# A one-core transformer layer: four engines' loops run four iterations a turn in place of two

## What is computed

```python
h = _L0_tok_ref(L0_tok_log_dt, x, L0_tok_B, L0_tok_inv_A_real, L0_tok_A_imag, 1024)      # (64, 128, 1024)
h = jnp.concatenate([jnp.broadcast_to(cls_tok, (h.shape[0], 1, h.shape[2])), h], axis=1)
h = h + _L0_attn_ref(_layernorm(h, axis=-1), ...)
h = h + _L0_ffn_ref(_layernorm(h, axis=-1), ...)

# inside _L0_attn_ref, with h of width 128
h = gelu(x @ w_down.T + b_down)          # exact gelu
xmid = h
h = _hydra(h, *hp); h = _hydra(h, *hp)
h = xmid + (alpha * xmid + (1.0 - alpha) * h)
return x_init + (h @ w_up.T + b_up)

# inside _L0_ffn_ref
base_out = x @ base_W.T + base_b
w = top-8 softmax weights of x @ router_W.T + router_b, mapped to 8 experts
lora = ((x @ A) * w) @ Bm * 2.0
```

## Time and profile before

| | us |
|---|---|
| median of 3 runs | 2546.23 |
| lowest, highest | 2546.2, 2549.94 |
| the profiled execution | 2549.21 |
| its span, first to last instruction | 2547.5 |

### The profile page before, as it was taken

How to read it: one execution, slowest core, us unless ns; L and a number is a source line. 1 busy time by engine, 2 the same in 40 slices (tenths; PEclk the granted TensorE clock), 3 DMA queues, 4 the chain that set the end, 5 groups by cost and what they waited for, 6 DMA issues and landing times.

```text
span 2547.5 us, 52475 instructions
## 1 busy us (share of the span) xinstructions
PE 2236.7 (88%) x14117; PEld 1838.9 (72%) x14117; DVE 1993.2 (78%) x5213; ACT 1529.7 (60%) x2926; POOL 1038.7 (41%) x1365
## 2 busy tenths in 40 slices
PE   1136799999999999999999999999999999999998
PEld 1125577777777777777777777777777777777776
DVE  6846788888878788888888787888888888878664
ACT  3435576666666666666666666666666666666652
POOL 2634444444444344444444343444444443434321
PEclk9966699999999999999999999999999999999999
DMA  3211011111111111111111111111111111111211
GB/s 102 71 34 33 33 52 37 59 58 58 58 38 49 58 58 58 55 31 58 58 58 58 38 49 58 58 58 55 32 58 58 58 58 38 49 58 57 63 36 31
DMA packets 90062, 132.62 MB, mean 52 GB/s; under 512 B 20379, under 2 KB 63559, under 8 KB 90006
## 3 DMA queue, kind: packets, MB, share of 16 engines
q1 hardware_dynamic: 79176, 125.60, 16.6%
q10 hardware_dynamic: 10830, 6.35, 0.9%
HBM read 55.17 MB, written 76.74 MB: 52 GB/s over the span
## 4 chain that ended last, share of the span: by engine, by line
PE 35%; DVE 23%; issue 21%; ACT 12%; DVEq 2%; POOL 1%; ACTq 1%; DMA 0%; SPq 0%; POOLq 0%
PE bank L1457 8%; PE bank L1556 5%; DVE sp_x L1129 3%; DVE NF L1192 3%; DVE NF L1198 3%; PE bank L1661 3%; PE bank L1546 3%; ACT T L877 3%; ACT CX L892 2%; DVE W L1157 2%; ACT SQ L975 2%; DVEq L47 2%; PE bank L1512 2%; PE bank L1487 2%; PE bank L1499 2%
## 5 line engine op out<-in xcount | busy, mean ns | idle before, releaser
L1457 PE MATMUL bank<-w_hi,XHI 128*128 128x512 f32 (+1 forms) x1560 | 629.2, 403 | 1.4 <-DVE XLO L1348 1.4
L1457 PE MATMUL bank<-w_lo,XHI 128*128 128x512 f32 (+1 forms) x1560 | 554.3, 355 | 0.0
L1457 PE MATMUL bank<-w_hi,XLO 128*128 128x512 f32 (+1 forms) x1560 | 553.9, 355 | 0.0
L1095 DVE SCALAR_TENSOR_TENSOR CX<-bank,cw,CX 128x252 f32<-128x252 f32 (+5 forms) x804 | 342.9, 461 | 100.8 <-ACT CX L892 100.8
L877 ACT ACTIVATE T<-bank 64x512 f32<-64x512 f32 x256 | 151.8, 593 | 352.8 <-PE bank L1546 348.2
L1457 PEld LDWEIGHTS bank<-w_hi,XLO 128*128 128x128 f32 x1560 | 295.6, 189 | 46.4
L1457 PEld LDWEIGHTS bank<-w_hi,XHI 128*128 128x128 f32 x1560 | 296.5, 190 | 38.3 <-DVE XLO L1348 1.7
L1457 PEld LDWEIGHTS bank<-w_lo,XHI 128*128 128x128 f32 x1560 | 296.3, 190 | 38.1
L849 POOL TENSOR_TENSOR CB<-CB,CM 48x252 f32<-48x252 f32 (+5 forms) x402 | 267.6, 666 | 137.9 <-ACT CM L877 109.2
L792 POOL TENSOR_TENSOR NB<-GB,sp_dt 128x512 f32<-128x512 f32 x67 | 100.3, 1496 | 297.4 <-DVE GB L1175 297.4
L813 POOL TENSOR_TENSOR RS<-VE,half_neg 128x1 f32<-128x1 f32 x65 | 35.6, 547 | 409.7 <-DVE VE L1292 409.7
(11 more groups left out here) (296 smaller groups left out, 5786.9 us busy)
## 6 DMA issues: line engine op xcount, KB each, us to landing
carried<-T SPq DMA_DIRECT2D x65, 512.0 KB, 4.7
T<-carried SPq DMA_DIRECT2D x65, 512.0 KB, 3.9
out<-HB SPq DMA_DIRECT2D x129, 256.0 KB, 3.2
tables<-tab SPq DMA_DIRECT2D x8, 560.0 KB, 4.1
TB<-tables SPq DMA_DIRECT2D x64, 70.0 KB, 2.8
carried<-U SPq DMA_DIRECT2D x65, 64.0 KB, 3.6
XM<-carried SPq DMA_DIRECT2D x65, 64.0 KB, 4.7
XI<-in_x SPq DMA_DIRECT2D x128, 32.0 KB, 2.8
```

The source lines that it names most:

```text
L1095: inc(STT(CX[:, c, :, s:CS], src[:, :, 0:CS - s], cw[:, c, k:k + 1], CX[:, c, :, s:CS], ALU.mult, ALU.add), "conv")
L1457: ins = mm(bank[:, 0:c1 - c0], xs_[:, 1 - p, k, :], ws[:, k, c0:c1], start=(c0 == HID and k == 0 and n == 0), stop=(last == k and n == 2))
```

## The change

`iterations` takes the number of iterations a turn as an argument, 2 unless given. GpSimd, ScalarE, VectorE and TensorE ask for 4, SP stays at 2. The loop's end moves from 62 to 60, for all five, so that its range is a multiple of 4 (52 iterations: 13 turns of four, and 26 of two on SP). Iterations 60 and 61 are now written out.

```diff
-        LOOP_FROM, LOOP_TO, LAST = 8, CLS - 2, TILES + 5
-        assert CLS % 2 == 0 and LOOP_TO > LOOP_FROM
-
-        def iterations(eng, body):
+        LOOP_FROM, LOOP_TO, LAST = 8, CLS - 4, TILES + 5
+        assert CLS % 4 == 0 and LOOP_TO > LOOP_FROM
+
+        def iterations(eng, body, unroll=2):
 
             for i in range(LOOP_FROM):
                 body(i, i % 2)
-            with eng.Fori(LOOP_FROM, LOOP_TO, 2) as m:
-                for u in range(2):
-                    body(m + u, u)
+            with eng.Fori(LOOP_FROM, LOOP_TO, unroll) as m:
+                for u in range(unroll):
+                    body(m + u, u % 2)
             for i in range(LOOP_TO, LAST):
                 body(i, i % 2)
...
-                iterations(pool, body)
+                iterations(pool, body, 4)
...
-                iterations(act, body)
+                iterations(act, body, 4)
...
-                iterations(dve, body)
+                iterations(dve, body, 4)
...
-                iterations(pe, body)
+                iterations(pe, body, 4)
```

## The result

| | us, median | lowest to highest |
|---|---|---|
| before | 2548.09 | 2546.20 to 2550.21, 4 runs |
| after | 2597.32 | 2594.64 to 2599.02, 4 runs |
| ratio | 1.0192 | 95% interval 1.0174 to 1.0210 |

The change makes the kernel slower by 49.2 us. The sign is the forecast's, the size is not: 2559 was predicted, and 2597 lies 21 us above the upper end of the range. (Before has one run more here than where the forecast started, 2546.23.)

A forecast was written before the change was run, and what follows sets the result against it. No engine fills the span; waits between engines bound the kernel, with a path through VectorE. A gain of -20.6 us and fetch stalls of +33.6 make +13.0, on the median of 2546.23 a forecast of 2559 us, range 2523 to 2576.

The forecast's parts named there:

- 12 x 2.8 us = +33.6: Branches back: each of 12 waits 2.8 us for code to be fetched, +33.6 us; with 1.7 to 4.2 us, 20 to 50.
- the gain: Loop iterations: only one of four keeps the wait for `down` ahead of the table load, and two become written-out: -20.6 us.
- I take 2.8 us: Price of fetching one block at a branch back, taken from the smallest block transfer, 32 KB with 2.8 us.
- the clock isn't a term here: TensorE: its granted clock is at its upper level, 2.4 GHz, from the sixth slice on, so no time was counted.
- ScalarE's fetch is covered for the most part: ScalarE at the branch back: it waits 1.19 us for TensorE there anyway, so its fetch is mostly hidden.
- The price is the longest stall, not the sum: Branch back: the engines' fetches run beside one another, so VectorE's stall alone sets the cost, 12 x 2.8 us.
- 3.5 was said: Sign on VectorE: at the branch back GF would start some 3.5 us after XLO in place of 0.70.
- (a): Rival: the doubled loops stay in the engines without fetches, only the gain is left, 2525.6 us, down to 2523; chance 0.20.
- (b): Rival: code is fetched cheaply; 1.3 to 2.1 us a branch gives 2541 to 2551 us, below 1.3 a gain; chance 0.20.
- (c): Rival: third and fourth iterations cost as the first and second, no gain, stalls on top, 2580 us; chance 0.02.
- 2.6 blocks stay, 5.0 perhaps not: VectorE's code: the old loop's 328 instructions, 2.6 blocks, stay; whether the changed loop's 5.0 stay no row shows.

The follow-up runs named there:

- e7: The kernel before with 64 long-fulfilled waits put ahead of VectorE's loop of two, no loop instruction changed: 2685.75 us against 2546.84, ratio 1.0542.
- e1: The kernel before with TensorE's loop alone at four iterations a turn, loop end at 60 for all: 2613.57 us against 2548.9, ratio 1.0251.
- e6: The kernel before, loops of two, with one more fulfilled wait on ScalarE, so the wait for `down` stands behind the table load: 2519.41 us against 2548.9.
- e4: ScalarE's loop alone at four, moved by 14 instructions by fulfilled waits ahead of it, against the kernel before: 2534.56 us against 2548.9, ratio 0.9946.
- e8: All 70 iterations written out on TensorE, VectorE, ScalarE and GpSimd, against the kernel before: 2504.03 us against 2546.84, ratio 0.9830.
- e2: The kernel before with VectorE's loop alone at four iterations a turn, loop end at 60 for all: 2611.07 us against 2546.84, ratio 1.0248.
- e3: The kernel before with ScalarE's loop alone at four iterations a turn, loop end at 60 for all: 2604.01 us against 2548.9, ratio 1.0218.

## Why the prediction was wrong in size and right in sign

**The step that failed** is the term "12 x 2.8 us = +33.6". It measured 12 x 5.4 = 65, above even the 50 us of the upper bound. Besides, the gain was some 16 us and not 20.6. With the gain left at 20.6 the term would be 12 x 5.8 = 70. Three things were off in it.

First, the stall itself. "I take 2.8 us", the median of a small transfer from issue to landing. The rows give 3.0 us of idle time on TensorE, 3.3 on ScalarE, 3.6 to 3.7 on VectorE when it is alone; GF is late by 3.17 at the branch back shown. That is within the bounds that were named (1.7 to 4.2 us), and makes up about 5 of the 36 us by which the sum was short (12 x 0.4). Another 5 are the gain.

Second, and most of it, "the clock isn't a term here". That was read off a kernel without such stalls. A stall of this length leaves TensorE nearly without work (0.53 us in 3), and behind each the granted clock is at its lower level for 3.4 or 6.8 us. What comes behind the stall is the rest of the 5.4, 2.2 us in the change, 27 us in all, and 1.4 in e7. At the branch back shown, L1630 alone takes 1.5 us longer, on the chain. With the longer dip the interval is 1.7 us longer than with the shorter in the change, and 1.6 in e1. An estimate from these: 1.5 everywhere and 1.7 more at five of twelve is 2.2, so the clock can make up all of it. It stays an estimate, since no run keeps the stall and prevents the dip.

Third, "ScalarE's fetch is covered for the most part". It is so for the first block, not for the second, of which the prediction knew nothing. In the change it doesn't show as a loss of its own, since the others stand still too. Alone it costs as much as theirs: the long interval is 41.3 us in the mean, 5.4 over 35.95, where 0.5 was expected.

**Right, by the same steps.** The old loops are fetched never, the new ones at each of twelve branches back, on q14 and on q8 too ("perhaps"). "The price is the longest stall, not the sum": the change loses 5.4 us a branch, TensorE alone 5.4, VectorE alone 5.3. The gain: the third and fourth iterations are 34.42 and 34.33 us (34.3 was said), the wait at L1032 is there 13 times, and e6, e4 and e8 have what that mechanism promises, each within 8 us. GF comes 3.8 us after XLO at the least (3.5 was said).

**The rivals.** (a), the loops stay, falls by the queues' packets. (b), a cheap fetch, falls by 5.4 against its 2.1, and by the stall of 3.0 alone. (c) falls by the intervals.

**What the rows could have told.** The prediction compared lengths: 2.6 blocks stay, 5.0 perhaps not. Which loops stay, in the nine kernels of this study that have loops on these engines, follows another count. Instructions are numbered in the built program, some 65 ahead of them (an offset fitted to the times of the packets), and cut into blocks of 128, for TensorE of 256:

| loop | instructions | blocks touched | fetched in the loop |
|---|---|---|---|
| VectorE, before, and moved by 128 | 328 | 3 | no |
| VectorE, moved by 64 | 328 | 4 | yes |
| ScalarE of two, before | 186 | 3 | no |
| ScalarE of four | 360 | 4 | yes |
| ScalarE of four, moved by 14 | 360 | 3 | no |
| GpSimd of four | 207 | 3 | no |
| VectorE of four | 645 | 6 | yes |
| TensorE of two | 916 | 4 | no |
| TensorE of four | 1823 | 8 | yes |

The packets speak for this count. A turn of the loops that are fetched has as many as the loop touches blocks, and one more: 5 for ScalarE of four, 5 for VectorE moved by 64, 7 for VectorE of four, 9 for TensorE of four. GpSimd adds none: from 470 to 2308 us the change has 150 packets on q14, e2 and e3 have 88 and 63. I take the one more to be the block behind the loop, asked for though it will not be used. If an engine keeps four blocks, and TensorE eight, a loop stays when its own and that one fit. That these are the stores' sizes is the model which fits all rows of the table, and not shown by itself; for TensorE the border lies somewhere between 4 and 8 blocks, and was not narrowed down. ScalarE's loop is a check on it without the fitted offset. For 360 instructions to touch four blocks of 128, and three when moved by 14, the loop must begin within the last 14 places of a block; the second stall of e3 says the same, that the target's block holds few of its instructions. The Trainium skill, page Runtime: NRT & Kernel Launch, section Instruction fetch mechanics, has 512 instructions for an engine and 2048 for TensorE, which is the same in sum (4 x 128, 8 x 256). Its blocks of 16 KiB don't agree with q14's packets of 8 KB, and in blocks of 8 KB its window of two for the target of a branch doesn't agree with the first row, which touches three and has no packet in 1838 us. Nor is it enough to be under the page's size: 1823, 360 and 328 instructions are, and were fetched.

## What to carry to other kernels

Unrolling a loop trades its branches, 0.09 us each here, for code, and a loop that no longer stays costs 5 to 6 us at each branch back, so count the blocks that each engine's loop touches, plus the one behind it, and look for packets in the instruction queues before and after. Where a loop alternates between a fast and a slow iteration, find the instruction that differs (here one wait ahead of a table load) and mend that alone; it gave 29 us where the unrolling lost 49. If code has to stream, let it stream straight: written out in full, the same work was 93 us faster than in the loop of four.

## What was unexpected of the hardware

- A block that is the target of a branch back and isn't there holds the engine for 3.0 us (TensorE, 16 KB) to 3.7 us (VectorE, 8 KB), though the packet of 8 KB takes some 0.3 us. In straight code such blocks cost nothing that the rows show (e8). These stalls fall where the data transfers are dense (DMA share 0.49 from 1417 to 1420 us in the change, 0.96 from 1238 to 1241 in e7). No run has a branch back at a quiet place, so what a fetch costs there is open.
- Alignment decides: 14 instructions ahead of a loop are worth 69 us, 64 ahead of another 139 us.
- Stalls of 3 to 3.7 us on any of three engines have TensorE's granted clock at 1.2 GHz for 3.4 or 6.8 us behind them (once 10.2, in e3), at each of 12 (26 in e7) places, though TensorE is busy 86 or 87% of the span.
- A fulfilled wait on VectorE isn't free: 128 of them with their empty instructions hold VectorE for 8.81 us, 69 ns each, and make the iteration 9.6 us longer (45.75 less 36.14 from U to U).
